# Attention on one NeuronCore: probabilities from key-major scores, with row maxima and inverse sums spread through DRAM

## The chip, the cores and the metric

One NeuronCore of a Trainium2 chip runs the whole program. The metric is the device time of one execution in microseconds, the median of several. Times within one execution come from a hardware profile: TensorE is PE (its weight loads PEld), VectorE is DVE, ScalarE is ACT, GpSimd is POOL, and SP is the sync engine that issues all DMAs.

## What is computed

Two layers over a batch of 16; the change touches the first only, a cross attention in float32.

```python
# hidden_states (16, 112, 512), audio_kv (16, 375, 512), 16 heads of 32
a = _layer_norm(audio_kv, ln_gamma, ln_beta)
Q = (hidden_states @ Wq.T).reshape(B, Tt, HEADS, HEAD_DIM).transpose(0, 2, 1, 3)
K = (a @ Wk.T).reshape(B, Ta, HEADS, HEAD_DIM).transpose(0, 2, 1, 3)
V = (a @ Wv.T).reshape(B, Ta, HEADS, HEAD_DIM).transpose(0, 2, 1, 3)
scores = jnp.einsum('bhtd,bhsd->bhts', Q, K) * scale
scores = jnp.where(mask, scores, jnp.float32(-jnp.inf))
attn = jax.nn.softmax(scores, axis=-1)
out = jnp.einsum('bhts,bhsd->bhtd', attn, V)
out = out.transpose(0, 2, 1, 3).reshape(B, Tt, D)
return hidden_states + jnp.tanh(gate) * (out @ Wo.T)
```

The second layer, an RWKV block over the same 16 x 112 rows, takes this result from DRAM.

## The kernel before

`cross_attention` is written in raw instructions: each engine has its own list, and semaphores order them. It is a software pipeline over the 16 batches. `run` calls `step(n, ...)` on every engine for n = 0 to 16; a step does three things side by side: it projects batch n (`project`), attends for batch m = n - 1 (`attend`), and finishes batch l = n - 2 (`finish`). `ln_stats` and `ln_apply` normalise the context of batch n + 1. Step 0 has nothing to attend, step 16 nothing to project. FIRST and LAST steps are written out, the middle ones are a hardware loop of two steps a turn.

The 16 heads go in four groups g of four heads (HG = 4, one head = 32 rows of K and Q). A group's way in the kernel before:

- `scores(m, g)` on PE: four matmuls, each on its own 32 rows, into the four banks `score_bank[0..3]`, rows = 112 queries, columns = 375 keys (row-major).
- `mask_scores` on DVE: one operation a head reads the bank, adds the mask, writes -scale x score to `probs`, and gives the row's minimum `least` (the negated maximum).
- `exps` on ACT: the exponential of each head in `probs`, with the row sum in `sums`.
- `transpose_probs` on PE: 12 transposes (3 tiles of 125 keys x 4 heads) into the ring; `copy_probsT` on ACT copies them to `probsT`, keys on partitions.
- `weigh_values` on PE: 12 matmuls, probabilities times values, into `av_bank`.
- `invert_sums` on DVE makes the inverse sums, each 32 wide in the row; `spread_inv` on PE turns two groups of them by a matmul with the identity, `copy_inv` copies them, and `scale_attn` on DVE multiplies two groups' results by them. `project_out`, `residual` and `store_x1` finish the batch.

The ring is three PSUM banks that PE fills and ACT empties in turn: context transposes T0 to T3, query q0 and q1, key projections K0 to K3, value projections V0 to V2, probability transposes P.., inverse sums I0 and I1. `free_unit` makes PE wait until the unit three places back has been copied. Key and value projections are split in high and low parts, three matmuls for each of four slices: 12 to a unit. They stand between the attention pieces in PE's list, so that other engines' work on a group is hidden. Within an engine the order is exactly that of `step`.

SP issues all transfers in order: a wait in its list holds every later one. Before, it issues per step the context (`load_ctx`, 125 partitions x 3 x 2 KB), x transposed, x by rows, and the store of x1. The weights for the second stage are loaded in steps 1 and 2 and its constants in step 3.

## Time and profile before

| | us |
|---|---|
| median of 3 runs | 1576.75 (1575.3 to 1579.61) |
| the profiled execution | 1575.7 |
| its span in the trace | 1573.9 |
| first to last scores of a first group | 48.0 to 628.4 |
| last x1 stored, first load of the second stage | 663.5, 666.2 |
| PE busy | 1444.3 |
| DVE, ACT busy | 929.1, 719.3 |

The page gives busy times over the whole span; what a change in the attention stage is worth is read from that stage's own rows. A timeline row gives the start, the duration from the first start to the last end of what it merges, and in brackets how long the engine sat idle before and for whom. Matmuls overlap, so that the distance between two rows' starts, not their duration, is what a piece costs PE.

### The profile page before, as it was taken

The page shows a single profiled execution, that of the slowest core. Times are in us where ns is not written, and L with a number is a line of the kernel's source. Part 1 is how long each engine was busy: PE and PEld are TensorE (multiplying, and loading weights), DVE is VectorE, ACT ScalarE, POOL GpSimd, SP SyncE. Part 2 cuts the span into 40 slices and gives each one's busy share as a digit, 9 for nine tenths or more (in the row PEclk, how much of TensorE's full clock was granted, in tenths as well). Part 3 has the DMA queues.
Part 4 walks back from the last instruction along what each step waited for, and adds up shares of the span by engine and source line. Part 5 has one row for each costly group of instructions (what it writes and reads, how often), then busy time and mean ns, then how long its engine had stood idle before and what let it go on. Part 6 is the DMA issues. An engine that isn't in the chain of part 4 may idle for free. (4 is left out here: it accounts for less than half of the span.)

```text
span 1573.9 us, 33178 instructions
## 1 busy us (share of the span) xinstructions
PE 1444.3 (92%) x12352; PEld 1081.0 (69%) x12352; DVE 929.1 (59%) x2287; ACT 719.3 (46%) x1772; POOL 469.1 (30%) x530
## 2 busy tenths in 40 slices
PE   4999999999999999668899999999999999999965
PEld 4777777777777777366667667666766676767632
DVE  2444444444444443327678787878777877887651
ACT  3666666666666666412433343334433443334312
POOL 1211111111111111024334532453245334533330
PEclk9999999999999999867999999999999999999977
DMA  7431111111111100020000000000000000000000
GB/s 202 146 86 39 38 38 38 37 37 37 37 37 37 37 12 13 18 113 13 18 25 6 20 24 25 9 16 25 24 18 8 24 25 18 8 24 19 18 6 12
DMA packets 25663, 54.59 MB, mean 35 GB/s; under 512 B 3984, under 2 KB 6672, under 8 KB 24016
## 3 DMA queue, kind: packets, MB, share of 16 engines
q1 hardware_dynamic: 25552, 52.99, 11.7%
q8 instruction: 85, 1.39, 0.4%
q14 instruction: 26, 0.21, 0.0%
HBM read 42.23 MB, written 7.34 MB: 31 GB/s over the span
## 5 line engine op out<-in xcount | busy, mean ns | idle before, releaser
L896 POOL TENSOR_TENSOR rst<-rp,st 128x448 f32<-128x448 f32 x192 | 195.2, 1041 | 67.9 <-DVE st L1092 67.9
L268 POOL TENSOR_TENSOR aT_lo<-whole,aT_hi 128x375 fp32r<-128x375 f32 x64 | 58.6, 916 | 450.0 <-ACT whole L420 447.1
L340 DVE CUSTOM_DVE_ANT_0 probs<-a_bank,unmask 112x375 f32<-112x375 f32 x256 | 125.9, 544 | 83.1 <-PE a_bank L537 72.4
L888 POOL TENSOR_TENSOR xm<-mixed,xa 128x448 f32<-128x448 f32 x80 | 84.9, 1077 | 301.7 <-DVE mixed L1021 274.0
L439 ACT ACTIVATE probs<-probs,least 112x375 f32<-112x375 f32 x256 | 153.8, 608 | 0.0
L346 DVE RECIPROCAL inv_rows<-sums 112x128 f32<-112x128 f32 x64 | 61.0, 953 | 156.1 <-ACT probs L439 156.1
L448 ACT COPY probsT<-a_bank 125x448 f32<-125x448 f32 x192 | 90.3, 536 | 53.2 <-PE a_bank L590 53.2
L590 PEld LDWEIGHTS a_bank<-ident_sb,probs 112*125 112x125 f32 x768 | 92.0, 190 | 31.1 <-ACT keyT L430 16.3
L1100 DVE TENSOR_TENSOR rst<-rp,st 128x448 f32<-128x448 f32 x64 | 109.7, 1715 | 0.0
L590 PE MATMUL a_bank<-ident_sb,probs 112*125 112x112 f32 x768 | 100.6, 281 | 3.4 <-ACT probs L439 3.4
L1021 DVE SCALAR_TENSOR_TENSOR mixed<-b_bank,vec_sb,sx 128x112 f32<-128x112 f32 x320 | 83.0, 325 | 31.9 <-PE b_bank L1537 31.6
L1592 PE MATMUL b_bank<-rst,b_collect 128*32 128x448 f32 x512 | 64.3, 571 | 34.7 <-DVE rst L1100 34.5
L535 PE MATMUL a_bank<-aT_hi,wk_lo 128*128 128x376 f32 x256 | 92.1, 360 | 2.4 <-ACT keyT L430 2.4
L1311 ACT COPY key<-b_bank 128x448 f32<-128x448 f32 x16 | 8.5, 533 | 186.4 <-PE b_bank L1485 186.4
L537 PE MATMUL a_bank<-aT_hi,wk_hi 128*128 128x376 f32 x256 | 85.9, 335 | 0.0
L536 PE MATMUL a_bank<-aT_lo,wk_hi 128*128 128x376 f32 x256 | 85.6, 334 | 0.0
L535 PE MATMUL a_bank<-wv_hi,aT_lo 128*126 128x512 f32 x192 | 79.8, 415 | 0.0
L537 PE MATMUL a_bank<-wv_hi,aT_hi 128*126 128x512 f32 x192 | 75.8, 395 | 0.0
L536 PE MATMUL a_bank<-wv_lo,aT_hi 128*126 128x512 f32 x192 | 75.7, 394 | 0.0
L1071 DVE TENSOR_TENSOR bv<-bv,ktil 128x392 f32<-128x392 f32 (+6 forms) x112 | 70.9, 633 | 3.9
L1491 PE MATMUL b_bank<-b_wo,rk 128*112 128x512 f32 x128 | 62.5, 634 | 8.7 <-POOL rk L915 8.7
L1485 PE MATMUL b_bank<-xk,b_wfk 128*128 128x112 f32 x512 | 64.3, 287 | 5.4 <-DVE xk L1154 5.4
(165 smaller groups left out, 3213.5 us busy)
## 6 DMA issues: line engine op xcount, KB each, us to landing
ctx_tok<-in_ctx SPq DMA_DIRECT2D x16, 750.0 KB
xT_sb<-in_xT SPq DMA_DIRECT2D x16, 224.0 KB, 9.7
x_tok<-in_x SPq DMA_DIRECT2D x16, 224.0 KB, 9.2
x_between_layers<-x_sb SPq DMA_DIRECT2D x16, 224.0 KB, 2.3
b_x<-x_between_layers SPq DMA_DIRECT2D x16, 224.0 KB, 2.8
x_post<-x_between_layers SPq DMA_DIRECT2D x16, 224.0 KB, 2.8
out_dram<-fin SPq DMA_DIRECT2D x16, 224.0 KB, 2.3
vbd<-vtok SPq DMA_DIRECT2D x208, 16.0 KB
```

The lines of the kernel that those rows point to most:

```text
L340: dve.tensor_tensor_reduce(out=probs[:, g % 2, i], in0=score_bank[i][0:T, 0:TC], in1=unmask[:, m[1]], scale=-SCALE, scalar=-LOWEST, op0=AL ...
L439: act.activation(probs[:, g % 2, i], probs[:, g % 2, i], ACT.Exp, scale=-1.0, bias=least[:, g % 2, i:i + 1], accum_out=sums[:, g % 2, i:i ...
L448: act.copy(probsT[:, g % 2, k], unit_bank(n, f"P{g}{k}")[0:TK, 0:HG * T]).then_inc(s_ringev, 1)
L535: pe.matmul(dst, ll, rh, start=start, stop=False)
L536: pe.matmul(dst, lh, rl, start=False, stop=False)
L537: return pe.matmul(dst, lh, rh, start=False, stop=stop)
L590: last = pe.transpose(dst[0:TK, i * T:(i + 1) * T], probs[:, g % 2, i, k * TK:(k + 1) * TK], ident[0:T, 0:T])
L888: pool.tensor_tensor(xm[:, f % 2], mixed[:, f % 2], xa[:, :, 1:T + 1], ALU.add).then_inc(s_xm, 1)
L896: pool.tensor_tensor(by_chunk(rst[:, j % NPROD]), by_chunk(rp[:].rearrange("p c t -> p (c t)")), state_of(j), ALU.mult).then_inc(s_pprod, 1)
L1021: last = dve.scalar_tensor_tensor(out=mixed[:, f % 2, c], in0=src[:, c * T:(c + 1) * T], scalar=vec[:, VEC[MIXES[f]], c:c + 1], in1=sx[:, ...
L1071: dve.tensor_tensor(dst, dst, vprod[:, :, 0:CH - d], ALU.add).then_inc(s_acc, 1)
L1100: dve.tensor_tensor(by_chunk(rst[:, j % NPROD]), by_chunk(rp[:].rearrange("p c t -> p (c t)")), state_of(j), ALU.mult).then_inc(s_vprod, 1)
```

## The change

The transposes go. The scores are computed a second time, key-major: `key_major_scores(m, g)` on PE makes 12 matmuls of 32 rows, with K as the stationary operand (125 keys) and Q moving (112 columns), into the same four banks as the row-major scores, which are now one tensor `score_bank[P, HG, BANK]`. `shift_scores` on DVE reads them in three operations, scales them and adds the row's `least`, which it needs along the free axis on all 125 key partitions. `exps_key_major` on ACT takes the exponential in place, with the key mask as bias; no copy of transposed tiles is left. The row-major way stays for the maximum and the sum.

`least` reaches the 125 partitions through DRAM: `spread_least` on SP waits for `mask_scores`, writes the 112 x 4 numbers transposed (4-byte pieces), waits for the write, and issues a read that is broadcast over the partitions. `spread_inv` does the same for the inverse sums of two groups: one write of 112 x 8 numbers and four reads, one for each 32 partitions. `invert_sums` now inverts 112 x 8 numbers for two groups.

The banks are shared by both kinds of scores, so `scores(m, 2)` waits for `shift_scores(m, 0)`, `scores(m, 3)` for `shift_scores(m, 1)`, `key_major_scores(m, g)` for `mask_scores(m, g + 1)`, and so on. The ring has twelve units (one q, no P, no I). `weigh_values(m, 3)` moves to the start of the next step, `project_out` behind the query projection. The context is loaded two batches ahead, at the end of SP's step; the weights for the second stage come one in each of the steps 0 to 3, the constants in step 14. A mask by keys is loaded at the start (`key_mask8`, 125 x 16 x 3 single bytes, behind the gate) and turned into additive numbers by POOL, which also copies one batch's part in each step.

```diff
+            def spread_least(m, g):
+                sp.wait_ge(s_masked, count(m, HEADS, (g + 1) * HG))
+                sp.dma_start(least_in_dram(m, g).rearrange("(i t) -> t i", t=T), least[:, g],
+                             allow_slow_non_contiguous=True).then_inc(s_least_out, 16)
+                sp.wait_ge(s_least_out, 16 * count(m, C, g + 1))
+                sp.dma_start(least_cols[:, g % 2], least_in_dram(m, g).rearrange("(o f) -> o f", o=1).broadcast_to([TK, HG * T])).then_inc(s_least_in[g % 2], 16)
+
+            def spread_inv(m, half):
+                sp.wait_ge(s_inv, count(m, 2, half + 1))
+                sp.dma_start(inv_in_dram(m, half).rearrange("g (i t) -> t (g i)", t=T),
+                             inv_rows[:, 2 * half:2 * half + 2].rearrange("t g i -> t (g i)"),
+                             allow_slow_non_contiguous=True).then_inc(s_inv_out, 16)
+                sp.wait_ge(s_inv_out, 16 * count(m, 2, half + 1))
+                for i in range(HG):
+                    sp.dma_start(inv_cols[i * HD:(i + 1) * HD, half].rearrange("p (g t) -> p g t", t=T),
+                                 inv_in_dram(m, half)[:, i * T:(i + 1) * T].rearrange("(o g) t -> o g t", o=1).broadcast_to([HD, 2, T])).then_inc(s_inv_in[half], 16)
...
+                m, l = later(n, -1), later(n, -2)
+                if attend:
+                    spread_least(m, 0)
+                    load_xtok(m)
+                    spread_least(m, 1)
                 if normalise and not is_batch(n, 0):
-                    load_ctx(later(n, 1))
                     load_x(later(n, 1))
-                if attend:
-                    load_xtok(later(n, -1))
-                if is_batch(n, 1):
+                if finish:
+                    store_x1(l)
+                if attend:
+                    spread_least(m, 2)
+                    spread_inv(m, 0)
+                    spread_least(m, 3)
+                    spread_inv(m, 1)
+                if normalise and not is_batch(n, B - 2):
+                    load_ctx(later(n, 2))
+                if is_batch(n, 0):
                     sp.wait_ge(s_wlo, 2 * C)
-                    for name in EARLY:
+                for name, at in zip(EARLY + AHEAD, (0, 1, 2, 3)):
+                    if is_batch(n, at):
                         sp.dma_start(W[name][:], A["b_" + name]).then_inc(w_loaded[name], 16)
-                if is_batch(n, 2):
-                    for name in AHEAD:
-                        sp.dma_start(W[name][:], A["b_" + name]).then_inc(w_loaded[name], 16)
-                if is_batch(n, 3):
+                if is_batch(n, B - 2):
                     load_constants()
-                if finish:
-                    store_x1(later(n, -2))
...
+            def shift_scores(m, g):
+                dve.wait_ge(s_least_in[g % 2], 16 * count(m, 2, g // 2 + 1))
+                if g >= 2 or at_least(m, 1):
+                    dve.wait_ge(s_av, count(m, C, g - 1))
+                dve.wait_ge(s_scoreT, count(m, C, g + 1))
+                for k in range(KT):
+                    dve.scalar_tensor_tensor(out=probsT[:, g % 2, k].rearrange("p (i t) -> p i t", t=T), in0=score_bank[0:TK, :, k * T:(k + 1) * T],
+                                             scalar=SCALE, in1=least_cols[:, g % 2].rearrange("p (i t) -> p i t", t=T),
+                                             op0=ALU.mult, op1=ALU.add).then_inc(s_shifted, 1)
+
+            def invert_sums(m, half):
+                dve.wait_ge(s_exp, count(m, HEADS, (2 * half + 2) * HG))
+                if at_least(m, 1):
+                    dve.wait_ge(s_inv_out, 16 * count(m, 2, half - 1))
...
+                if attend:
+                    mask_scores(m, 1, range(HG))
                 if normalise:
                     ln_stats(later(n, 1))
-                if attend:
-                    invert_sums(m, 0)
                 if finish:
                     residual(l)
                 if attend:
-                    mask_scores(m, 1, range(HG))
+                    shift_scores(m, 0)
+                    invert_sums(m, 0)
+                    mask_scores(m, 2, range(HG))
+                    shift_scores(m, 1)
+                    mask_scores(m, 3, range(HG))
+                    scale_attn(m, 0)
+                    shift_scores(m, 2)
+                    invert_sums(m, 1)
                 if normalise:
                     ln_apply(later(n, 1))
                 if attend:
-                    invert_sums(m, 1)
-                    mask_scores(m, 2, range(HG))
-                    scale_attn(m, 0)
-                    invert_sums(m, 2)
-                    mask_scores(m, 3, range(HG))
-                    invert_sums(m, 3)
+                    shift_scores(m, 3)
...
+                    act.wait_ge(s_shifted, count(m, C * KT, g * KT + k + 1))
+                    act.activation(probsT[:, g % 2, k], probsT[:, g % 2, k], ACT.Exp, bias=key_mask[:, m[1], k:k + 1]).then_inc(s_expT, 1)
...
+                elif g == 1:
+                    pe.wait_ge(s_masked, count(m, HEADS, HG))
+                else:
+                    pe.wait_ge(s_shifted, count(m, C * KT, (g - 1) * KT))
...
+            def key_major_scores(m, g):
+                if g < C - 1:
+                    pe.wait_ge(s_masked, count(m, HEADS, (g + 2) * HG))
+                else:
+                    pe.wait_ge(s_shifted, count(m, C * KT, g * KT))
...
-                        pe.wait_ge(s_exp, count(m, HEADS, (g + 1) * HG))
                     for i in range(HG):
-                        last = pe.transpose(dst[0:TK, i * T:(i + 1) * T], probs[:, g % 2, i, k * TK:(k + 1) * TK], ident[0:T, 0:T])
-                    last.then_inc(s_ring, 1)
+                        rows = slice(i * HD, (i + 1) * HD)
+                        last = pe.matmul(score_bank[0:TK, i, k * T:(k + 1) * T], keyT[rows, m[1], g, k * TK:(k + 1) * TK],
...
+                    pe.wait_ge(s_expT, count(m, C * KT, g * KT + k + 1))
...
+                if finish:
+                    weigh_values(l, 3)
+                if project:
+                    for c in range(C):
                         transpose_ctx(n, c)
+                if attend:
+                    scores(m, 1)
+                if project:
+                    project_query(n)
                 if finish:
                     project_out(l)
-                if project:
-                    transpose_ctx(n, 3)
-                    project_query(n, 0)
-                    project_query(n, 1)
-                if attend:
-                    scores(m, 1)
-                    transpose_probs(m, 0)
+                if attend:
+                    key_major_scores(m, 0)
                 if project:
                     project_key(n, 0)
                 if attend:
+                    scores(m, 2)
                     weigh_values(m, 0)
                 if project:
                     project_key(n, 1)
                 if attend:
-                    scores(m, 2)
-                    transpose_probs(m, 1)
+                    key_major_scores(m, 1)
                 if project:
                     project_key(n, 2)
                 if attend:
+                    scores(m, 3)
                     weigh_values(m, 1)
-                    spread_inv(m, 0)
                 if project:
                     project_key(n, 3)
                 if attend:
-                    scores(m, 3)
-                    transpose_probs(m, 2)
+                    key_major_scores(m, 2)
                 if project:
                     project_value(n, 0)
```

Where the instructions stand. First PE, from the last scores of a step into the next step. Before, it read (`a_bank` is the score, ring or value bank; L580 scores, L602 weighing, L610 inverse sums, L529 context transposes, L619 output projection):

```order
544 L610 MATMUL a_bank<-ident_sb,inv_rows 128x112 x2
545 L521 ISA
546 L527 REGISTER_ALU
547 L529 MATMUL a_bank<-ident_sb,ctx_norm 128x125 x3
548 L521 REGISTER_ALU
549 L529 MATMUL a_bank<-ident_sb,ctx_norm 128x125 x3
550 L521 REGISTER_ALU
551 L529 MATMUL a_bank<-ident_sb,ctx_norm 128x125 x3
552 L615 REGISTER_ALU
553 L619 MATMUL a_bank<-wo_sb,attnT 112x512 x4
554 L521 REGISTER_ALU
555 L529 MATMUL a_bank<-ident_sb,ctx_norm 128x125 x3
```

and now (behind the weighing of group 3 and the first of the context transposes; L572 context transposes, L625 row-major scores of group 1, L611 query, L658 output, L636 key-major scores):

```order
533 L572 MATMUL ring_bank<-ident_sb,ctx_norm 128x125 x6
534 L564 REGISTER_ALU
535 L572 MATMUL ring_bank<-ident_sb,ctx_norm 128x125 x3
536 L620 ISA
537 L625 MATMUL score_banks<-keyT,query 112x375 x4
538 L564 REGISTER_ALU
539 L611 MATMUL ring_bank<-xT_sb,wq_sb 128x112 x16
540 L654 REGISTER_ALU
541 L658 MATMUL av_bank<-wo_sb,attnT 112x512 x4
542 L630 REGISTER_ALU
543 L636 MATMUL score_banks<-query,keyT 125x112 x12
```

The output projection stood between the third and the fourth context transpose; it now stands behind scores and query, with the key-major scores of group 0 behind it.

Second SP, within the loop. Before (L197 context, L202 and L207 x, L211 store):

```order
39 L197 ISA
40 L197 DMA ctx_tok<-in_ctx 125x3x512
41 L201 ISA
42 L202 ISA
43 L202 DMA xT_sb<-in_xT 128x448
44 L206 ISA
45 L207 ISA
46 L207 DMA x_tok<-in_x 112x512
47 L211 ISA
48 L211 DMA x_between_layers<-x_sb 112x512
```

and now, from the store of x1 to the fourth group (L222 and L225 maxima out and in, L229 and L234 inverse sums out and in; ISA rows are waits):

```order
82 L218 DMA x_between_layers<-x_sb 112x512
83 L221 REGISTER_ALU
84 L222 DMA values_of_two_batches<-least 112x4x1
85 L224 ISA
86 L225 DMA least_cols<-values_of_two_batches 125x448
87 L228 ISA
88 L229 DMA values_of_two_batches<-inv_rows 112x8x1
89 L232 REGISTER_ALU
90 L234 DMA inv_cols<-values_of_two_batches 32x2x112 x4
91 L221 REGISTER_ALU
92 L222 DMA values_of_two_batches<-least 112x4x1
```

Four issues a step became twenty-two, each read behind the landing of its write; the inverse sums of the first two groups stand between the maxima of groups 2 and 3.

Third DVE, behind the masking of group 3. Before, the inverse sums' scaling stood behind the masking of group 2 (L351 scaling, L346 reciprocal, L338 and L340 masking):

```order
96 L340 ISA least 112x1
97 L351 TENSOR_TENSOR attnT<-a_bank,inv_cols 128x224
98 L346 RECIPROCAL inv_rows<-sums 112x128
99 L338 MEMSET score_seen 1x1
100 L340 ISA probs,least<-a_bank,unmask 112x375
```

and now (L390 masking, L413 scaling, L400 shift, L408 reciprocal, L373 normalisation):

```order
106 L390 ISA probs,least<-score_banks,unmask 112x375
107 L390 ISA least 112x1
108 L413 TENSOR_TENSOR attnT<-av_bank,inv_cols 128x224
109 L400 SCALAR_TENSOR_TENSOR probsT<-score_banks,least_cols 125x448 x3
110 L408 RECIPROCAL inv_rows<-sums 112x8
111 L373 TENSOR_SCALAR ctx_norm<-ctx_tok,ctx_meanvar,ctx_rstd 125x512 x3
112 L400 SCALAR_TENSOR_TENSOR probsT<-score_banks,least_cols 125x448 x3
```

Two shifts, the reciprocal and the normalisation are now queued behind the scaling of the first half.

## Rows read from the trace of the kernel before

**Rows 1.** Page, part 1 (busy us, share) and part 2 (tenths of 40 slices).
```profile
PE 1444.3 (92%) x12352; PEld 1081.0 (69%) x12352; DVE 929.1 (59%) x2287; ACT 719.3 (46%) x1772; POOL 469.1 (30%) x530
...
PE   4999999999999999668899999999999999999965
...
PEclk9999999999999999867999999999999999999977
```

**Rows 2.** Windows: one step, busy us of each engine, granted clock, DMA share.
```profile
core 0: us, PE busy (x) PEld busy (x) DVE busy (x) ACT busy (x) POOL busy (x), PEclk, DMA share, GB/s
343.30:382.20 38.90, 38.90 (x321) 30.56 (x320) 16.58 (x56) 24.50 (x63) 7.37 (x9) 1.00 0.12 37
```

**Rows 3.** Waits, 100 to 600 us: who waited for whom, us, times, longest.
```profile
DVE inv_rows L346 <- ACT probs L439: 131.2, 52, 5.6
...
PEld a_bank L590 <- ACT keyT L430: 14.1, 26, 0.5
```

**Rows 4.** Timeline of PE, 300 to 345 us: start, us, what.
```profile
306.54 0.48 PE L535 MATMUL a_bank<-wv_hi,aT_lo 128*126 128x512 f32 x1
...
309.48 0.78 PE L602 MATMUL a_bank<-probsT,value 125*32 125x112 f32 x24
...
319.42 1.14 PE L529 MATMUL a_bank<-ident_sb,ctx_norm 125*128 125x125 f32 x9
320.44 3.69 PE L619 MATMUL a_bank<-wo_sb,attnT 128*112 128x512 f32 x8
323.96 0.48 PE L529 MATMUL a_bank<-ident_sb,ctx_norm 125*128 125x125 f32 x3
324.29 3.73 PE L570 MATMUL a_bank<-xT_sb,wq_sb 128*128 128x112 f32 x32
327.94 0.90 PE L580 MATMUL a_bank<-keyT,query 32*112 32x375 f32 x8
328.77 1.56 PE L590 MATMUL a_bank<-ident_sb,probs 112*125 112x112 f32 x12
...
335.45 0.90 PE L580 MATMUL a_bank<-keyT,query 32*112 32x375 f32 x8
336.28 1.56 PE L590 MATMUL a_bank<-ident_sb,probs 112*125 112x112 f32 x12
337.61 0.43 PE L535 MATMUL a_bank<-aT_hi,wk_lo 128*128 128x376 f32 x1
...
339.84 0.78 PE L602 MATMUL a_bank<-probsT,value 125*32 125x112 f32 x24
340.56 0.70 PE L610 MATMUL a_bank<-ident_sb,inv_rows 112*128 112x112 f32 x4
341.02 0.42 PE L535 MATMUL a_bank<-aT_hi,wk_lo 128*128 128x376 f32 x1
```

**Rows 5.** Lines, 0 to 720 us: the row-major scores, busy us, mean ns.
```profile
L580 PE MATMUL a_bank<-keyT,query 32*112 32x375 f32 x512 | 57.5, 519 | 0.0
```

**Rows 6.** Timelines of ACT and DVE, 290 to 345 us.
```profile
320.06 0.66 ACT L416 ACTIVATE aT_hi<-a_bank,vec_sb 128x375 fp32r<-128x375 f32 x1
...
321.17 0.66 ACT L416 ACTIVATE aT_hi<-a_bank,vec_sb 128x375 fp32r<-128x375 f32 x1
...
337.00 1.41 ACT L448 COPY probsT<-a_bank 125x448 f32<-125x448 f32 x3 [0.98 <-PE a_bank L590]
338.31 0.61 ACT L439 ACTIVATE probs<-probs,least 112x375 f32<-112x375 f32 x1
...
327.86 0.65 DVE L361 SCALAR_TENSOR_TENSOR x_sb<-a_bank,tanh_gate,x_tok 112x512 f32<-112x512 f32 x1
...
336.50 0.54 DVE L340 CUSTOM_DVE_ANT_0 probs<-a_bank,unmask 112x375 f32<-112x375 f32 x1 [1.26 <-PE a_bank L537]
...
338.37 0.08 DVE L340 DVE_READ_ACCUMULATOR2_ANT least<- 112x1 f32 x1
```

**Rows 7.** Timelines of SP and DVE from 663 us: a store, a load, its consumer.
```profile
663.51 0.33 SPq L211 DMA_DIRECT2D x_between_layers<-x_sb  x1
666.20 0.32 SPq L817 DMA_DIRECT2D b_x<-x_between_layers  x1
...
668.71 0.69 DVE L983 BATCH_NORM_STATS2 ln_bn<-b_x 112x6 f32<-112x512 f32 x1 [5.22 <-DMA b_x<-x_between_layers]
```

**Rows 8.** Timeline of SP from 1012 us: thirteen small copies issued in a row.
```profile
1012.58 8.68 SPq L832 DMA_DIRECT2D vbd<-vtok  x13
```

**Rows 9.** Page, part 6 (KB each, us to landing); window within a context load.
```profile
ctx_tok<-in_ctx SPq DMA_DIRECT2D x16, 750.0 KB
xT_sb<-in_xT SPq DMA_DIRECT2D x16, 224.0 KB, 9.7
...
b_x<-x_between_layers SPq DMA_DIRECT2D x16, 224.0 KB, 2.8
...
373.00:375.50 2.50, 2.50 (x19) 1.72 (x18) 1.02 (x3) 0.66 (x3) 0.00 (x0) 1.00 0.33 125
```

**Rows 10.** Timeline of PE, 600 to 672 us: last projections' end, pauses of step 16.
```profile
628.40 0.90 PE L580 MATMUL a_bank<-keyT,query 32*112 32x375 f32 x8
...
645.94 1.53 PE L590 MATMUL a_bank<-ident_sb,probs 112*125 112x112 f32 x12 [0.88 <-ACT probs L439]
648.09 0.78 PE L602 MATMUL a_bank<-probsT,value 125*32 125x112 f32 x24 [0.62 <-ACT probsT L448]
650.55 2.83 PE L590 MATMUL a_bank<-ident_sb,probs 112*125 112x112 f32 x12 [1.68 <-ACT probs L439]
```

## What I predict, and how it follows

> **What bounds the kernel now.** I read the views in this order: busy shares by slice, the windows of a stretch, the waits, then one step of the attention stage on every engine in order of time. In the page, TensorE (PE) is busy 92% of the span and its tenths are 9 through the whole attention stage [rows 1]. A window of one step shows PE 38.90 us busy of 38.90 at the full clock (1.00, the 2.4 GHz level), with DVE at 16.58 and ACT at 24.50 us [rows 2]. The waits of that stretch are all on the other engines: POOL, DVE and ACT wait for PE or for one another, and PE's weight loads wait 14.1 us in total for ring buffers [rows 3]. So one step costs what PE executes in it, 38.9 us, and there are 15 of them between the first scores at 48.0 us and the last at 628.4 us. The second stage (from 666 us on) is not touched, and I carry it over.
>
> The PE timeline gives each piece as a distance between starts [rows 4]. Scores of four heads: 335.45 to 336.28, 0.83 us. Twelve transposes: 1.33 us (1.47 us at 328.77, before a first key projection). A key projection: 337.61 to 339.84, 2.23. Weighing values: 339.84 to 340.56, 0.72. Spreading the inverse sums: 0.46. A value projection with its transposed neighbour: 306.54 to 309.48, 2.94. Output projection: 320.44 to 323.96, 3.52. Three context transposes: 0.33. Query: 324.29 to 327.94, 3.65.
>
> **What goes from PE, and what comes.** Gone are four groups of transposes, 1.47 + 3 x 1.33 = 5.5 us, and two spreads of the inverse sums, about 1.0 us with the gap behind them: 6.5 us a step. Added are four key-major score groups of twelve matmuls. No row shows that shape. Nearest from below is the weighing, also 24 records with 112 moving columns, in which four tiles run side by side: 0.72 us. From above, 32 records of the query projection with as wide a stationary tile, one after the other, take 3.65 us, so 24 would take 2.7. The scores settle it: L580 has the same split over four row groups, and 8 records whose mean is 519 ns [rows 5] fit in 0.83 us. Four are therefore in flight. I take 0.75 a group, 3.0 a step. PE's own floor becomes 38.9 - 6.5 + 3.0 = 35.4 us.
>
> One cover goes away. The output projection stood between the third and the fourth context transpose, whose bank ACT must empty first. ACT needs 1.1 us for one such copy pair, from 320.06 to 321.17 [rows 6], and in the new order only the rest of three short transposes stands before it: 0.9 us of wait. So 36.3 us.
>
> ACT loses twelve copies of 0.47 us (1.41 for three) and gains twelve exponentials of the same tile; rows give 0.51 to 0.61 us for 375 columns [rows 6], so I take 0.6: 24.5 becomes about 26 us. DVE loses four reciprocals of 0.95 us and gains twelve reads of 125x448 from PSUM. The residual's 112x512 read takes 0.65 us [rows 6], so about 0.57 each, 6.9 in all: 16.6 becomes about 20 us. Neither becomes the bound by its sum. Their cost is one of order.
>
> **What is added as a wait: the round trips through DRAM.** SP writes a group's maxima, waits, reads them back over 125 partitions; for the inverse sums it writes, waits and issues four reads. Prices, from rows: the last x1 of this stage is issued at 663.51 as a store and the next load, which waits for all stores, at 666.20, 2.7 us later; its consumer starts at 668.71, 2.5 us after its issue [rows 7]. Those move 224 KB with 16 transfer engines. Thirteen small copies are issued in 8.68 us, 0.67 each [rows 8].
>
> The write of the maxima is 448 pieces of 4 bytes, that of the inverse sums 896. No row shows such pieces. Lower bound: the 2.7 us of the store. Upper bound: a piece costs as much as one of the context load's 2 KB pieces. That load has 375 pieces, and keeps 0.33 of 16 engines busy, that is 5 [rows 9]; x, queued behind it, lands 9.7 us after its issue instead of the 2.8 us of a load by itself [rows 9]. So 75 pieces an engine in about 8 us, 0.1 us a piece: 28 pieces an engine make 2.8 us more, 56 make 5.6 more. Bounds: 2.7 to 5.5 us and 2.7 to 8.3 us. I take 3.0 and 3.6, near the lower end, since pieces of 4 bytes should be nearer to the fixed part than to 2 KB. The read of the maxima is 125 rows of 1792 bytes. It has the partition count of the context load, so I let it use 5 engines too, 25 rows each: 2.5 us plus 17 rows more than the 8 of a 16-engine load, at about 0.08, 3.8 us to its consumer.
>
> The Trainium skill, *DMA: Bandwidth & Descriptors* (Why a DMA increments its semaphore by 16 and not by 1), says that the number of engines is the largest divisor up to 16 of the slowest dimension: 5 for 125 partitions. The 0.33 in the row agrees. The same page (Rules for kernel authors) says that a strided last dimension becomes one descriptor per element and advises against it. No row here shows what that costs; it speaks for the upper bound, which is priced below as a rival.
>
> **The chain that ends last.** Take the PE start of scores(m,2) as zero. The first mask starts 1.05 later and the fourth ends at 3.0 (335.45, 336.50 and 338.45) [rows 4, 6]. SP writes the maxima at 3.1 and issues their read at 6.1. Only then comes the inverse sums' write: 6.7, whose four reads start at 10.3 and end issue at 12.3; the last serves its consumer at 14.6. scale_attn(m,0) waits for it on DVE, and behind it are queued shift_scores(m,2), invert_sums(m,1), the normalisation and shift_scores(m,3). Scaling 0.4, three shifts 1.7, the last exponential 0.7: the last third of weigh_values(m,2) starts at 17.4 and ends at 17.7. PE's own work to there is 0.83 + 0.72 + 2 x 2.23 + 0.75 + 0.83 + 0.72 + 2.23 + 0.75 + 2.94 + 0.72 = 14.95. PE waits 2.8 us. A step is 36.3 + 2.8 = 39.1 us, against 38.9: everything saved is paid back.
>
> The other transfers have slack in this count. The first maxima of a step are queued behind the context load of the step before, some 7 us on 5 engines. They are back about 2 us before shift_scores(m,0), which has to wait for the output projection and the residual anyway.
>
> **Sum.** 15 steps at +0.2: +3. Three of the first steps end with a 1 MB weight load ahead of the next maxima (4 us on all engines against 2 us of slack): +6. The last step has no projections to hide anything. Before, it takes from 628.40 to 663.5, 35 us [rows 4, 10]; now two round trips (maxima 6.8, inverse sums 8) stand on its path in place of transposes and copies, which I put at 41: +6. Together +15. Profiled run 1575.7 us (span 1573.9 and 1.8 around it), median of the runs 1576.75: 1591.
>
> **Rivals.** (a) *Cheap pieces, PE stays the bound.* If writes land as the store does and each issue is 0.1 us quicker, the chain is 1.3 us shorter; if also the reads are quicker, all 2.8 us go. Time: 15 x (36.3 to 37.9 - 38.9) = -39 to -15, with +3 in the tail: 1540 to 1564. For it: nothing in the trace makes small pieces dear, and PE loses 3.5 us of work. Against: it needs three serial transfers faster than the only measured pair.
>
> (b) *The serial SP queue becomes the bound.* It does so from the point at which SP's own sum passes the step. A maxima trip holds SP for 3.0 + 0.6, an inverse trip for 3.6 + 2.6, four other DMAs for 2.4: 14.4 + 12.4 + 2.4 = 29 us of 39. At the upper bounds it is 24.4 + 21.8 + 2.4 = 49 us; then a step is at least 49, +10 x 15: 1727. Halfway (4.1 and 5.6 us) it is 38.6 us plus the waits between them, and the chain grows by 3.1: a step of 42.2, time about 1640. The skill's advice above speaks for this one.
>
> (c) *The clock falls.* PE now pauses for 2.8 us in one place. In the last step before, pauses of 0.6 to 1.7 us between short bursts were followed by transposes of 2.83 us instead of 1.53 [rows 10], the 1.2 GHz level. One such stretch of 2 us lost in each step: +30 on the sum, 1621.
>
> (d) *The key mask, loaded byte by byte* (6000 pieces on 5 engines) holds the second and third context. At 0.015 us a piece it is hidden; at the 0.1 of the upper bound it ends 120 us on, and the first steps lose some 70 us: 1660.
>
> **How the numbers follow.** Central case 0.38 (1570 to 1605), (a) 0.27, (b) with its halfway form 0.18, (c) 0.12, (d) 0.05. The range leaves out the top of (b) and the lower part of (a): 1550 to 1655. About 0.3% (5 us) is what a measurement here can tell from no change. Faster: all of (a) and 0.05 of the central case, 0.32. Same, 1572 to 1581.5: 0.11. Slower: 0.57.
>
> **What would show it.** The key-major groups at 0.75 us each and PE's busy sum near 36 us a step. PE's longest wait before weigh_values(m,2), released by ACT's exponentials; DVE's before scale_attn(m,0), released by the inverse columns' DMA, about 28 us into the step. Maxima writes that land in 2.5 us; 5 transfer engines busy in the read. Wrong would be: PE 100% busy (then (a)), SP waiting for its own writes most of the time (b), a granted clock under 1 in the middle of the stage (c), or a first step far longer than the others (d).

## The result, and the profile after

The changed kernel takes 2155.23 us (median of four runs, 2150.94 to 2156.02) where the one before takes 1577.97 on the same chip: ratio 1.3655, 95% interval 1.3631 to 1.3678. I had predicted 1591, with 1655 as the top of the range. It is slower, as forecast, but by 577 us and not by 15. The page's parts 1 and 2, beside [rows 1]:

```profile
span 2153.7 us, 34866 instructions
...
PE 1546.9 (72%) x12992; PEld 1113.5 (52%) x12992; DVE 979.2 (45%) x2447; ACT 727.6 (34%) x1724; POOL 472.4 (22%) x550
...
PE   6456556566656666656565258999999999999976
...
PEclk9677787887878877777886578999999999999988
```

The attention stage now fills 23 of the 40 slices; PE's tenths fell there from 9 to mostly 5 or 6, its clock from 9 to 7 or 8 in most slices. The windows between the first and the last group of row-major scores, of the kernel before (596 us) and of the one after (1145 us), one fence each:

```profile
45.00:641.00 596.00, 592.11 (x4877) 462.79 (x4876) 253.04 (x835) 374.93 (x967) 109.98 (x134) 1.00 0.14 42
```

```profile
45.00:1190.00 1145.00, 693.25 (x5496) 496.46 (x5496) 305.72 (x999) 386.27 (x930) 112.41 (x151) 0.77 0.21 40
```

549 of the 580 us of span are lost here: 15 steps, from one first group's scores to the next, went from 38.9 us [rows 2] to 72.8 (the middle one; 70 to 84), which is 530 us, and the beginning of a last one got longer with them. Another 27 us are lost between the last scores and the last x1; the second stage is as long as before, within about 4 us. No engine is anywhere near busy: PE works 693 of 1145 us. So something is waited for, and it is the queue that issues the transfers. Its waits over the whole run (us in total, times, longest):

```profile
SPq L225 <- DMA values_of_two_batches<-least: 579.6, 63, 17.4
SPq L234 <- DMA values_of_two_batches<-inv_rows: 324.1, 32, 13.0
```

SP stands 904 us before L225 and L234, the reads, until its own writes (L222 of the maxima, L229 of the inverse sums) are complete. One step on SP, start and length of each issue:

```profile
509.53 0.30 SPq L222 DMA_DIRECT2D values_of_two_batches<-least  x1
518.50 0.27 SPq L225 DMA_DIRECT2D least_cols<-values_of_two_batches  x1
518.95 0.34 SPq L214 DMA_DIRECT2D x_tok<-in_x  x1
519.40 2.44 SPq L222 DMA_DIRECT2D values_of_two_batches<-least  x1
530.99 0.26 SPq L225 DMA_DIRECT2D least_cols<-values_of_two_batches  x1
531.51 0.36 SPq L209 DMA_DIRECT2D xT_sb<-in_xT  x1
532.05 2.31 SPq L218 DMA_DIRECT2D x_between_layers<-x_sb  x1
534.47 0.37 SPq L222 DMA_DIRECT2D values_of_two_batches<-least  x1
544.23 0.26 SPq L225 DMA_DIRECT2D least_cols<-values_of_two_batches  x1
544.61 0.32 SPq L229 DMA_DIRECT2D values_of_two_batches<-inv_rows  x1
554.46 1.73 SPq L234 DMA_DIRECT2D inv_cols<-values_of_two_batches  x4
556.30 0.35 SPq L222 DMA_DIRECT2D values_of_two_batches<-least  x1
563.73 0.27 SPq L225 DMA_DIRECT2D least_cols<-values_of_two_batches  x1
564.11 0.30 SPq L229 DMA_DIRECT2D values_of_two_batches<-inv_rows  x1
575.45 1.71 SPq L234 DMA_DIRECT2D inv_cols<-values_of_two_batches  x4
...
582.48 0.31 SPq L222 DMA_DIRECT2D values_of_two_batches<-least  x1
```

From one first maxima write to the next, 509.53 to 582.48, are 72.95 us. The four maxima writes hold SP for 8.97, 11.59, 9.76 and 7.43, the two inverse writes for 9.85 and 11.34: 58.9 us one behind the other. Over all steps the middle value is 9.7 us from write to read for the maxima (6.6 to 17.8, 64 writes) and 10.2 for the inverse sums (8.8 to 13.4, 32 writes). The other 14 us are other issues, and a stretch in which the queue has run empty. DVE and PE show the latter:

```profile
573.67 1.69 DVE L400 SCALAR_TENSOR_TENSOR probsT<-score_banks,least_cols 125x448 f32<-125x448 f32 x3 [12.40 <-DMA least_cols<-values_of_two_batches]
...
581.12 0.39 DVE L413 TENSOR_TENSOR attnT<-av_bank,inv_cols 128x224 f32<-128x224 f32 x1 [2.95 <-DMA inv_cols<-values_of_two_batches]
...
575.50 1.61 PE L625 MATMUL score_banks<-keyT,query 32*112 32x375 f32 x8 [5.97 <-DVE probsT L400]
...
582.51 0.90 PE L625 MATMUL score_banks<-keyT,query 32*112 32x375 f32 x8 [1.10 <-DVE least L390]
```

The last maxima of the step, whose read was issued at 563.73, reach the shift at 573.67. Only that shift frees the score banks for the next step's first scores (575.50), and in the middle of their masking DVE stands until 581.12 for the inverse columns. So the next maxima write cannot go before 582.48, and from 575.45 on no write is in flight. The read itself is slow here: 9.9 us from its issue to the shift.

What a write does in its 7.4 us is seen in two windows between the issues at 556.30 and 563.73, and what the last inverse write (564.11 to 575.45) does in two more, busy us of PE, PEld, DVE, ACT, POOL, then the granted clock, DMA share and GB/s:

```profile
556.40:558.10 1.70, 0.00 (x0) 0.00 (x0) 0.26 (x1) 0.00 (x0) 0.00 (x0) 0.50 0.39 68
558.10:563.70 5.60, 4.09 (x30) 2.69 (x31) 3.17 (x8) 2.25 (x4) 0.00 (x0) 0.50 0.00 0
566.00:573.00 7.00, 3.53 (x35) 2.54 (x28) 0.00 (x0) 0.33 (x1) 0.00 (x0) 1.00 0.21 25
573.70:575.40 1.70, 0.00 (x0) 0.00 (x0) 1.66 (x3) 1.07 (x2) 0.00 (x0) 0.77 0.00 0
```

Within 1.8 us of its issue the pieces of the maxima write have passed the transfer engines. In the next 5.6 us these move nothing at all (0.00), and still the write is not reported complete. The Trainium skill, *DMA: Bandwidth & Descriptors* (Anatomy of one DMA), says, of DMAs that GpSimd issues, that most of the fixed 2 us is the receipt of the target memory, for which the semaphore's update must wait. SP issues the ones here. The idle engines agree with where the time is spent; its size does not: 7.4 us.

The inverse write spends its 11.3 us otherwise. It was issued right behind the read of the maxima. The trace's packets show about 620 of its 896 pieces passing by 565.8, and the last 230 or so only between 573.0 and 573.6, with the last of the read's 125 rows. Completion came 1.8 us after that. So a wait before a read holds two things: the way of the pieces behind whatever stands before them on the transfer engines, and the completion. Worked out from the packets of all 16 steps, the completion alone (last piece passed to read issued) is 5.7 us at the middle for the maxima of group 3, and 1.8 us for the inverse sums behind them, whose last piece passes 9.7 us after the issue.

### The profile page after: what moved, and what is told of

The parts are those of the page before. It is cut to its first block and busy times, and to the rows that moved or that the text cites. A ratio compares the mean times of both kernels' runs of the same rounds, so it can differ in the third digit from the quotient of the medians.

```text
span 2153.7 us, 34866 instructions
## 1 busy us (share of the span) xinstructions
PE 1546.9 (72%) x12992; PEld 1113.5 (52%) x12992; DVE 979.2 (45%) x2447; ACT 727.6 (34%) x1724; POOL 472.4 (22%) x550
## 5 line engine op out<-in xcount | busy, mean ns | idle before, releaser
L625 PE MATMUL score_banks<-keyT,query 32*112 32x375 f32 x512 | 89.1, 779 | 291.6 <-DVE probsT L400 271.3
L510 ACT ACTIVATE probsT<-probsT,key_mask 125x448 f32<-125x448 f32 x192 | 114.3, 658 | 545.0 <-DVE probsT L400 545.0
L400 DVE SCALAR_TENSOR_TENSOR probsT<-score_banks,least_cols 125x448 f32<-125x448 f32 x192 | 107.8, 617 | 417.6 <-DMA least_cols<-values_of_two_batches 407.3
L649 PE MATMUL av_bank<-probsT,value 125*32 125x112 f32 x1536 | 88.8, 384 | 181.6 <-ACT probsT L510 181.6
L625 PEld LDWEIGHTS score_banks<-keyT,query 32*112 32x112 f32 x512 | 26.4, 244 | 311.7 <-DVE probsT L400 193.1
L390 DVE CUSTOM_DVE_ANT_0 probs<-score_banks,unmask 112x375 f32<-112x375 f32 x256 | 126.0, 545 | 63.9 <-issue 63.9
L413 DVE TENSOR_TENSOR attnT<-av_bank,inv_cols 128x224 f32<-128x224 f32 x32 | 12.5, 392 | 275.4 <-DMA inv_cols<-values_of_two_batches 275.4
L578 PE MATMUL ring_bank<-aT_hi,wk_lo 128*128 128x376 f32 x256 | 104.4, 408 | 0.1
L579 PE MATMUL ring_bank<-aT_lo,wk_hi 128*128 128x376 f32 x256 | 93.7, 366 | 0.0
L580 PE MATMUL ring_bank<-aT_hi,wk_hi 128*128 128x376 f32 x256 | 92.6, 362 | 0.0
L578 PE MATMUL ring_bank<-wv_hi,aT_lo 128*126 128x512 f32 x192 | 89.7, 467 | 0.0
L579 PE MATMUL ring_bank<-wv_lo,aT_hi 128*126 128x512 f32 x192 | 83.1, 433 | 0.0
L580 PE MATMUL ring_bank<-wv_hi,aT_hi 128*126 128x512 f32 x192 | 82.1, 428 | 0.0
L611 PEld LDWEIGHTS ring_bank<-xT_sb,wq_sb 128*128 128x128 f32 x512 | 74.0, 234 | 11.4 <-issue 6.1
```

Source lines behind the costliest of these rows:

```text
L390: dve.tensor_tensor_reduce(out=probs[:, g % 2, i], in0=score_bank[0:T, i, 0:TC], in1=unmask[:, m[1]], scale=-SCALE, scalar=-LOWEST, op0=AL ...
L400: dve.scalar_tensor_tensor(out=probsT[:, g % 2, k].rearrange("p (i t) -> p i t", t=T), in0=score_bank[0:TK, :, k * T:(k + 1) * T], scalar= ...
L510: act.activation(probsT[:, g % 2, k], probsT[:, g % 2, k], ACT.Exp, bias=key_mask[:, m[1], k:k + 1]).then_inc(s_expT, 1)
L578: pe.matmul(dst, ll, rh, start=start, stop=False)
L579: pe.matmul(dst, lh, rl, start=False, stop=False)
L580: return pe.matmul(dst, lh, rh, start=False, stop=stop)
```

## The experiments

The first experiments ask two things: is it the round trips at all, and do the pieces cost by their number or by how they lie in DRAM? A kernel whose time is given below without an interval was executed once.

**no_trips.** Both helpers return before they issue anything; VectorE shifts and scales by constants.

```
 def spread_least(m, g):
-    sp.wait_ge(s_masked, count(m, HEADS, (g + 1) * HG))
+    return
```

> The changed kernel without any round trip: maxima and inverse sums on the key side are constants set once, so the output is not the attention. PE, DVE and ACT do all their work. If the round trips alone make the loss, a step is 36 to 37 us (the 36.3 us of the prediction), the granted clock is back at 1.0 and the time about 1540 us, below the kernel before. If the new order of PE, DVE and ACT costs something of its own, the step stays above 38.9 us and the time above 1576.

1560.89 us. A window in the middle of the stage:

```profile
400.00:500.00 100.00, 97.99 (x986) 73.26 (x985) 53.08 (x175) 67.18 (x158) 18.60 (x24) 1.00 0.11 35
```

PE is busy 98 of 100 us at the full clock. Its only wait from 100 to 600 us is the one before the context transposes, 0.67 us a step. A step is 37.1 us; the total is 21 us over the 1540 I had expected. So all of the 594 us by which the changed kernel lies above this one are due to the trips; the second set of scores is cheap.

**dense and spaced.** In both, the reads take a row of constants. `dense` keeps the maxima's writes as they are. `spaced` writes the same 448 pieces of 4 bytes 64 bytes apart:

```
-sp.dma_start(least_in_dram(m, g).rearrange("(i t) -> t i", t=T), least[:, g], ...)
+sp.dma_start(A["v"][m[1], 16 + 16 * g:32 + 16 * g].rearrange("r c -> (r c)")
+             .rearrange("(i t x) -> t i x", t=T, i=HG)[:, :, 0], least[:, g], ...)
```

> The changed kernel, but the broadcast reads of the maxima take a constant row stored once at the start, while the 4-byte writes go on as they are; this leaves the row maxima out of the probabilities. A control for the next run. If the slow part is the completion of the writes, the time stays near 2155 us, and issue to next issue at a maxima write stays near 9.7 us. If it is the reading of numbers that were just written, the reads get quicker and the time falls by over 50 us.

> As dense, but the 448 pieces of 4 bytes are stored 64 bytes apart instead of side by side. Theory A (pieces that fall into the same stretch of DRAM hold one another up): a maxima write comes back in about 3 us instead of 9.7, a step shortens by some 20 us and the time falls to about 1850 us. Theory B (each piece has its price wherever it goes, about 15 ns): the write still takes 8 to 10 us, the time stays near 2155.

`dense` 2026.03 us, `spaced` 1709.43. SP's waits in the two kernels, first `dense`, then `spaced`:

```profile
SPq L225 <- DMA values_of_two_batches<-least: 562.1, 64, 17.6
```

```profile
SPq L225 <- DMA values_of_two_batches<-least: 201.2, 64, 11.7
```

The same number of pieces of the same size: 9.0 us from write to read at 4 bytes apart, 3.15 us at 64. From the last piece's passage to the read it is 5.8 us in `dense` and 0.6 in `spaced` (maxima of group 3, middle of 16). Number and size don't make the price; the place in DRAM does.

`dense` shows a second price. Its writes are those of the changed kernel and it is still 129 us faster, which was the sign I had set for slow reads of numbers that were just written. The same place as 563.73 and 573.67 above, and as 519.40 and 532.05, in `dense`:

```profile
509.54 0.27 SPq L225 DMA_DIRECT2D least_cols<-values_of_two_batches  x1
...
516.82 1.69 DVE L405 SCALAR_TENSOR_TENSOR probsT<-score_banks,least_cols 125x448 f32<-125x448 f32 x3 [9.82 <-DMA least_cols<-values_of_two_batches]
...
533.56 0.36 SPq L222 DMA_DIRECT2D values_of_two_batches<-least  x1
...
544.80 0.33 SPq L218 DMA_DIRECT2D x_between_layers<-x_sb  x1
```

Where the shift waits for its read, it starts 6.2, 7.1 and 10.1 us after the read's issue in the changed kernel (groups 0, 1 and 3, middle values) and 4.3, 4.6 and 6.4 us in `dense`. The inverse writes, which stand behind such reads, come down from 10.2 to 8.7 us, and of the 24 issues of maxima writes and x1 stores over 1 us, 4 are left. Whether it matters that the numbers are fresh or that they were written in 4-byte pieces, no run separates.

**rows16.** The maxima go out token by token, four heads in one piece of 16 bytes; the shift reads them with a stride of four.

```
-sp.dma_start(least_in_dram(m, g).rearrange("(i t) -> t i", t=T), ...)
+sp.dma_start(least_in_dram(m, g).rearrange("(t i) -> t i", i=HG), least[:, g])
...
-in1=least_cols[:, g % 2].rearrange("p (i t) -> p i t", t=T)
+in1=least_cols[:, g % 2].rearrange("p (t i) -> p i t", i=HG)
```

> The changed kernel with the maxima stored query by query: 112 pieces of 16 bytes side by side instead of 448 of 4; the shift reads them with a stride. The inverse sums are as they were. By number of pieces (theory B) the write comes back in about 2 + 5.8/4 = 3.5 us; if neighbours in DRAM hold one another up (theory A), 4 neighbours in 64 bytes instead of 16, about the same 3.5 us. Either way four writes lose 6 us each: a step of about 50 us and a time near 1800 us.

1721.73 us, where I had expected about 1800; 2.7 us from write to read. The step is about 46 us. Two changed lines take 433 us off, and still leave 9 us a step above `no_trips`.

**rows16_32 and rows_wide.** The inverse sums go out as rows of 32 bytes too, come back in one read and are scaled in four operations; `rows_wide` also reads the maxima into 128 partitions instead of 125.

> Both kinds of write go out as rows: the maxima as 112 pieces of 16 bytes, the inverse sums as 112 pieces of 32 bytes, and the inverse sums come back by one read of 128 x 896 in place of four, scaled by four operations. The output is the reference's. Theory A (what costs is how neighbouring small pieces in DRAM complete, and it costs because all trips stand in one queue): the maxima trips stay at 2.7 us, the inverse trips fall from 7.85 to about 2.7 us, the queue then has some 16 us of trips in a step and no longer sets its length, and the step comes near TensorE's floor: 38 to 41 us, a total of 1575 to 1620 us. Rival (the inverse trips are not on the path, the fast steps of 46 us are set by the chain shift, exponential, weighing): the total stays within 20 us of the 1721.73 of the kernel with 16-byte rows for the maxima alone.

> As the kernel before it in this list, and the maxima are read back over 128 partitions in place of 112, so that the pieces of the read spread over more than the five transfer engines that carried it. Output as the reference. If the read's length over five engines (packets of 0.08 us each or more, 22 or 23 behind each other on an engine) is on the path of the step, each of the 64 reads lands about 1 us earlier and the total falls by 15 to 60 us against the kernel before it in this list; if TensorE is the bound there by then, nothing changes: within 8 us of it.

1699.82 us (ratio to before 1.0764, interval 1.073 to 1.0798) and 1692.10 (1.0721, 1.0679 to 1.0763). Here my theory missed by 80 us, and the rival by 2. The wider read gains nothing clear: 7.7 us, with runs of 1692 to 1705 in the one kernel and 1685 to 1697 in the other. The trips did fall as expected, to 2.2 and 2.65 us in the second kernel, but the queue had stopped being the bound at 46 us a step: it now waits 295 us for the masking on DVE. Something else holds the step at 45. The lines of DVE in `rows_wide`, the shift and the scaling:

```profile
L397 DVE SCALAR_TENSOR_TENSOR probsT<-score_banks,least_cols 125x448 f32<-125x448 f32 x192 | 171.8, 952 | 112.2 <-PE score_banks L636 106.7
...
L412 DVE TENSOR_TENSOR attnT<-av_bank,inv_cols 32x224 f32<-32x224 f32 x128 | 72.0, 563 | 29.1 <-DMA inv_cols<-values_of_two_batches 26.4
```

A shift takes 952 ns, where the changed kernel's take 617: 12 x 0.335 = 4.0 us a step. Four scalings of 563 ns stand for one of 392, twice a step: 3.7 us. (I had put the partitions of the read at 112 in these expectations; the tile has 125.)

**no_trips_strided** asks whether that is the reason: `rows_wide` without any trip.

> No trip through DRAM at all, constants in place of maxima and inverse sums, so not the attention of the reference; VectorE's operations are those of the kernels with rows of 16 and 32 bytes: the shift takes its second operand with a stride of four elements (0.95 us each in place of 0.62) and the scaling is done in four operations of 32 partitions. The kernel without trips and without these strides took 1560.89 us, the kernel with both row-wise writes 1692 us. If VectorE's longer operations are what keeps the latter at 45 us a step, this one has steps over 41 us and takes over 1625 us. If the trips' latency does it, it stays at 37 to 39 us a step and 1560 to 1590 us.

1637.75 us, steps of 40.5 to 44 us after the first. Of the 131 us between `no_trips` and `rows_wide`, 77 come from DVE's longer operations and 54 from what is left of the trips. The Trainium skill, *SBUF — State Buffer* (Specifications (TRN2)), says that SBUF is read in lines of 16 bytes and that an access which leaves its line each time pays for it. A stride of 16 bytes does so with every element, and the 952 ns agree.

**no_least_trips and no_inv_trips.** One kind of trip alone.

> The 64 trips of the maxima are left out and the shift takes a constant instead, so this is not the attention of the reference; the 32 trips of the inverse sums stay as in the changed kernel, 4-byte pieces and four reads. Serial-queue theory: two trips of about 9 us in a step leave the queue idle half of the time, TensorE is the bound, and the total is 1561 to 1600 us. Rival (the inverse trip is itself on the path: sums, reciprocal, 10 us of trip, scaling, projection): scale_attn waits for its columns and pushes the projection out, 3 to 6 us a step, 1610 to 1660 us.

> The 32 trips of the inverse sums are left out and the scaling takes a constant, so this is not the attention of the reference; the 64 trips of the maxima stay as in the changed kernel. Serial-queue theory: the step of 72.5 us loses the two trips of 10.2 us in the queue and their waits, and some of what they do to the maxima's trips; 45 to 52 us a step and a total of 1690 to 1800 us. Rival (only the maxima lie on the path, the inverse trips have hidden in the queue's idle time): the total stays within 5 per cent of 2155 us.

1571.29 and 1782.90 us, both as the serial queue has it. Two trips of 6.5 us (they are shorter when no maxima are in flight) fit under a step of PE: 10 us above `no_trips` in all, 8 of them in the first four steps. Four maxima trips of 8.4 us alone make a step of 51.

**overlap.** The changed kernel with another order in the queue, nothing else:

```
-spread_least(m, 2)
-spread_inv(m, 0)
-spread_least(m, 3)
-spread_inv(m, 1)
+for half in range(2):
+    write_least(m, 2 + half)
+    write_inv(m, half)
+    read_least(m, 2 + half)
+    read_inv(m, half)
```

> Pieces and bytes are those of the changed kernel, and the output is the reference's. Only the order in the queue that issues them is another: in the second half of a step the write of the inverse sums goes out right behind the write of the maxima, before the queue waits for either, and the two reads follow. If the time comes from waits that stand one behind the other in one queue (a step of 72.5 us = 4 trips of 9.7, 2 of 10.2, and some 11 us in which the queue is empty between the last read of a step and the first maxima of the next), two of the six waits now lie under others: 54 to 60 us a step, 1850 to 1960 us in all. If the time comes from a rate at which such pieces can be completed (448 and 896 of them, whoever waits), the two writes in flight together take as long as one after the other, and the total stays within 3 per cent of 2155 us.

1910.64 us (1.2102, interval 1.2057 to 1.2147). SP in a step of it (L226 and L231 write and read the maxima, L235 and L242 the inverse sums):

```profile
608.74 0.36 SPq L226 DMA_DIRECT2D values_of_two_batches<-least  x1
609.24 0.46 SPq L235 DMA_DIRECT2D values_of_two_batches<-inv_rows  x1
619.66 0.27 SPq L231 DMA_DIRECT2D least_cols<-values_of_two_batches  x1
620.04 1.71 SPq L242 DMA_DIRECT2D inv_cols<-values_of_two_batches  x4
```

Both writes complete within 11 us, where one alone takes 10; in all 16 steps this pair takes 8.8 to 11.8 us. In the second half of a step the inverse write goes out 5.5 us behind the maxima's, since its sums come later, and the two take 15.4. So the delay is in the main a latency, not a rate, and what makes it 72.8 us a step is that six of them stand in one queue. Putting one under another, and a second partly, takes 245 us off, with the same pieces and bytes.

**wide.** Only the 128 partitions of the maxima's read.

> The changed kernel with one difference: the maxima are read back over 128 partitions in place of 112, which spreads the pieces of the read over more than five transfer engines. Output as the reference. The queue does not wait for this read to land, only for the writes; so if the queue's waits set the step, only the one place where the queue has run empty gains (the last maxima of a step, 6 us from the issue of the read to the shift): 1 to 3 us a step, a total of 2110 to 2150 us. If the reads are what delays the writes that follow them (their pieces stand ahead on the same engines), each of the four trips gets shorter by more than 1 us, and the total falls under 2090 us.

2046.59 us, 109 less: neither side had this. The reads got quicker, 4.9, 4.9 and 5.3 us from issue to shift where the changed kernel has 6.2, 7.1 and 10.1. Summed over the stage, the stretches from write to read are 74 us shorter (46.5 at the maxima, 27.6 at the inverse sums; 9.3 and 9.6 us at the middle), the store of x1 holds the queue 20 us less, and the stretch before a step's first maxima 13. Part of this is in the issues themselves; the same place as 519.40 and 532.05 above, in `wide`:

```profile
612.70 0.34 SPq L214 DMA_DIRECT2D x_tok<-in_x  x1
613.15 0.35 SPq L222 DMA_DIRECT2D values_of_two_batches<-least  x1
...
624.05 0.36 SPq L218 DMA_DIRECT2D x_between_layers<-x_sb  x1
```

0.35 and 0.36 us in place of 2.44 and 2.31: 4 us in this step. The few engines of the read are not enough for that: `dense` reads over the same 125 partitions and has 0.36 and 0.33. The long issues come mostly where such a read is slow as well, with a load behind it.

**spacings, prices_count, prices_order.** What does the completion hang on? In each, the maxima's write takes four forms in turn, 16 times each, and the reads take constants.

```
+if (g + 2 * m[1]) % 4 == 0:
+    sp.dma_start(head_rows(m, 0, 1), least[:, g], ...)          # 448 pieces side by side
+elif (g + 2 * m[1]) % 4 == 1:
+    sp.dma_start(head_rows(m, 1, 1)[:, 0:2], least[:, g, 0:2], ...)   # 224
+elif (g + 2 * m[1]) % 4 == 2:
+    sp.dma_start(head_rows(m, 2, 1)[:, 0:1], least[:, g, 0:1], ...)   # 112
```

> The reads take a constant row, so the maxima are left out and this is not the attention of the reference. The 64 writes of maxima have the same 448 pieces of 4 bytes as the changed kernel, and the distance of neighbouring pieces in DRAM is, in turn, 4, 16, 32 and 64 bytes, each on a line of its own, each 16 times. Known so far: 9.0 us from write to read at 4 bytes apart, 3.15 us at 64. If pieces hold each other up when they share one stretch of 64 bytes, the time falls with the number that share it (16, 4, 2, 1): 9, 5 to 6, 3.5 to 4.5, 3 us. If a stretch of 32 bytes is what counts, 32 and 64 give the same. If it were the total size of the area that is written, 16 bytes apart would be near 64 already. Total between 1750 and 1880 us.

> The reads take a constant row, so the maxima are left out and this is not the attention of the reference. The writes of maxima take four forms in turn, each 16 times, each on a line of its own: all 448 pieces of 4 bytes side by side; the 224 of two heads side by side; the 112 of one head side by side; and all 448, 8 bytes apart. Known: 7.75 us at the middle for 448 side by side, 3.5 us for 448 that are 16 bytes apart, 2.7 us for 112 pieces of 16 bytes. If pieces that touch each other are completed one after the other at a rate, the time falls with their number: about 7.75, 5, 3.5 us. If it is a delay that any such write meets, 224 and 112 stay over 6 us. At 8 bytes apart: near 3.5 us if only touching pieces matter, half-way (5 us) if the share of a small stretch does. Total 1720 to 1850 us.

> As the kernel before it in this list (constant row, not the attention), with four other forms of the write: 448 pieces 8 bytes apart in the order row by row (the four neighbours in DRAM come from one partition, so from one transfer engine); 448 pieces 8 bytes apart in the order head by head (neighbours come from different partitions); 448 pieces 16 bytes apart row by row; and the 112 rows of 16 bytes. If it matters that different transfer engines write into the same small stretch, the first form costs near 3 us and the second clearly more. If only the distance matters, the two are alike. The last two forms serve as anchors: 3 to 3.5 us and 2.2 to 2.7 us. Total 1700 to 1800 us.

They took 1782.10, 1949.82 (100 over the top of my range) and 1779.32 us. Time from the write's issue to the read's, us, worked out from SP's timeline:

| form of the write | pieces in 64 bytes | least | middle | kernel |
|---|---|---|---|---|
| 448 of 4 B, 4 B apart | 16 | 6.2 | 7.75 | spacings |
| 448 of 4 B, 4 B apart | 16 | 6.3 | 8.5 | prices_count |
| 224 of 4 B, 4 B apart | 16 | 6.5 | 8.3 | prices_count |
| 112 of 4 B, 4 B apart | 16 | 6.0 | 9.1 | prices_count |
| 448, 8 B apart, head by head | 8 | 3.0 | 4.6 | prices_count |
| 448, 8 B apart, head by head | 8 | 3.3 | 4.9 | prices_order |
| 448, 8 B apart, token by token | 8 | 3.6 | 5.5 | prices_order |
| 448, 16 B apart, head by head | 4 | 2.3 | 3.5 | spacings |
| 448, 16 B apart, token by token | 4 | 2.7 | 4.3 | prices_order |
| 448, 32 B apart | 2 | 1.8 | 2.9 | spacings |
| 448, 64 B apart | 1 | 1.9 | 3.2 | spacings |
| 112 of 16 B | 4 | 1.9 | 3.2 | prices_order |

The four forms of a kernel did not change places freely: the first and third always stood at groups 0 and 2 of a step, the second and fourth at groups 1 and 3, and the place alone moves the middle value (7.7 to 11.1 us in the changed kernel). So compare within a pair: in `prices_count` 448 with 112 pieces, 224 pieces with 8 B apart; in `spacings` 4 B with 32 B, 16 B with 64 B. Two stretches of `prices_count` for the reading: 112 pieces (L237) and 448 at 8 bytes (L240), each up to L242.

```profile
572.93 0.36 SPq L237 DMA_DIRECT2D values_of_two_batches<-least  x1
583.16 0.26 SPq L242 DMA_DIRECT2D least_cols<-values_of_two_batches  x1
...
593.57 0.35 SPq L240 DMA_DIRECT2D values_of_two_batches<-least  x1
597.84 0.27 SPq L242 DMA_DIRECT2D least_cols<-values_of_two_batches  x1
```

A quarter of the pieces costs as much as all: 10.2 us here. Twice the distance halves it: 4.3. Nor is it the size of the area: 112 pieces of 16 B fill the same 1792 bytes as 448 of 4 B side by side. Which partitions the neighbours come from changes less than the distance does (4.9 and 5.5 us, and these two stood at different places). The least values fall with how many pieces share a small stretch, about 0.3 us for each beyond two (6.2 - 1.8 over 14; 0.2 up to eight, 0.4 from there on), whatever their number in all. The middle values carry the rest of the traffic and the place in the step, and differ by up to 1 us between kernels. That is what one would see if the pieces of one stretch were completed one after another, and the stretches beside each other. It is an inference: nothing in a trace shows the memory's side. I expected 5 to 6 us at 16 bytes and got 3.5, so the size of the stretch stays open.

## Why the prediction was wrong

**The step that failed is the price of the trips, the writes above all.** I priced a piece by what it does on the transfer engines, and bounded it above by one of the context load's 2 KB pieces: 5.5 us for the maxima, 8.3 for the inverse sums. Measured are 9.7 and 10.2 at the middle. Every row I used was a load or a store of large pieces. There, the last piece's passage and the completion lie close together; [rows 7] gave 2.7 us. In the write at 556.30 the engines are done after 1.8 us and the completion comes 5.6 us later. So the upper bound was no bound: more of the quantity that I had rows for says nothing on one that I had none for. "Pieces of 4 bytes should be nearer to the fixed part" was an argument for the wrong quantity. The advice on strided last dimensions that I weighed (the Trainium skill, *DMA: Bandwidth & Descriptors*, Rules for kernel authors) pointed the right way, but one descriptor for each element is not what costs: with 64 bytes between pieces there are as many, at 3.15 us.

The read had its own error. I had 3.8 us to its consumer; it took 6.2 to 10.1 where the shift waited for it. What stood behind it paid too: part of the 10.2 us of an inverse write is that read's rows (without any maxima trip it was 6.5). `dense` puts a size on this part, 129 of the 577 us.

**The mechanism was rival (b)**, and its own test was met: SP waits for its own writes for 904 us. At the measured prices its sum would have been 4 x (9.7 + 0.6) + 2 x (10.2 + 2.6) + 2.4 = 69 us a step, against 72.8 measured. (Its halfway sum has a slip: 4.1 and 5.6 us give 37.6, not 38.6.) I had added the waits between them only in the halfway form. In its upper form I left them out, and that was the second, smaller error: a queue whose write needs the shift of its own last read runs empty once a step. I gave it 0.18 and cut the range at 1655, below the 1727 that its stated upper bound gave.

**The clock, rival (c)**, fell too, to 0.77, after PE's pauses: scores took 1.61 us (575.50) after an idle 5.97 us, 0.90 at 582.51, the levels of 1.2 and 2.4 GHz. In all, PE's work in the stage took 693 us instead of the 557 of `no_trips`. It is a result of the queue, since without trips the clock is 1.00 (400 to 500 us). How much of the 136 us lies under the waits no run separates.

**What held.** PE's floor: I had 36.3 us with the context's wait of 0.9; `no_trips` has 37.1 with 0.67. A key-major group costs 0.85 us and not 0.75, which is half of the 0.8 between them. The shift is 617 ns against 570, the exponential 658 against 600; the windows' sums from 549 to 622 us are 19.9 us for DVE and 23.4 for ACT, where I had 20 and 26. PE's longest single waits come before the weighing and are released by ACT's exponentials (10.43 us at 559.61), and DVE's by the columns, as listed. Not listed was the wait that is the largest in total, before the row-major scores, for the shift that frees their banks:

```profile
L625 PE MATMUL score_banks<-keyT,query 32*112 32x375 f32 x512 | 89.1, 779 | 291.6 <-DVE probsT L400 271.3
...
L400 DVE SCALAR_TENSOR_TENSOR probsT<-score_banks,least_cols 125x448 f32<-125x448 f32 x192 | 107.8, 617 | 417.6 <-DMA least_cols<-values_of_two_batches 407.3
...
L413 DVE TENSOR_TENSOR attnT<-av_bank,inv_cols 128x224 f32<-128x224 f32 x32 | 12.5, 392 | 275.4 <-DMA inv_cols<-values_of_two_batches 275.4
...
L649 PE MATMUL av_bank<-probsT,value 125*32 125x112 f32 x1536 | 88.8, 384 | 181.6 <-ACT probsT L510 181.6
```

The read on 5 engines held too: of the 896 pieces behind it about 620 passed at once, which is eleven engines' share at 56 each, and the rest with its rows, on the other five. `wide` showed its price, which I had left out. **Rival (d)** did not happen: behind the key mask SP stood 23 us, but the first scores came no later (44.15 us; before, 47.96).

```profile
18.16 0.61 SPq L258 DMA_DIRECT2D key_mask<-in_mask  x1
18.81 23.02 SPq L260 DMA_DIRECT2D wo_sb<-in_wo  x1
```

**Is there a version that beats both?** Not among these. The change without any trip is 1560.89, 1% under the kernel before, and that is the most it could give. With only the inverse sums through DRAM it was 1571.29, but then the maxima would need another way that costs PE and DVE nothing. The best that computes the attention is `rows_wide`, 7% slower than before. Not tried are trips issued from a second queue, and 16-byte rows whose operand DVE then reads without a stride.

## What to carry to other kernels

A round trip through DRAM is priced from the issue of the write to the issue of the read that waits for it, and from there to the read's consumer, and only a measured row of the same pattern bounds it; the time on the transfer engines does not. Count all such waits of one queue in a row, with the stretch in which its own results must come back before it can go on, and compare that sum with the step: six waits of 10 us in one queue cost more than everything that they replaced. If small values must go through DRAM, write them as contiguous rows, issue all writes that are ready before waiting for one, and look at what the new layout does to the engine that reads it.

## What the runs showed of the hardware

- From the issue of a write to DRAM in 4-byte pieces side by side to the issue of the read that waits for it are 6 us at the least and 8 to 9 at the middle, whether it has 112 or 448 pieces (`prices_count`). At 16 bytes or more apart it is 1.8 to 2.7 at the least and 2.9 to 4.3 at the middle (`spacings`, `prices_order`).
- Of this, 5.7 us in the changed kernel come after the last piece has passed, with the transfer engines at a share of 0.00; 0.6 us at 64 bytes apart (`spaced`).
- Two such writes issued 0.5 us apart complete in about the time of one (609.24 to 620.04 in `overlap`, 8.8 to 11.8 us in 16 steps).
- The broadcast read of 125 rows reaches its consumer in 6.2 to 10.1 us when its numbers were just written in 4-byte pieces, and in 4.3 to 6.4 when it reads a constant row (`dense`). Pieces of a write issued behind it pass after its rows.
- An issue on SP takes 0.3 us. Behind the slow read and a load it takes 2.4 us, with 0.36 where the read is of a constant row (`dense`) or spread over 128 partitions (`wide`). A load of bytes (6000 pieces) held the next issue for 23 us.
- VectorE with its second operand at a stride of 16 bytes takes 952 ns for 125x448, 617 ns without.
